# An adaptive-norm transformer block with routed experts: query tiles of the two rows interleaved, small vectors loaded as rows and turned, and the last results gathered by blocks

## What is computed

```python
mod = (silu(c) @ wmod).reshape(2, 6, 1, -1)      # per row: sa, ca, ga, sb, cb, gb
h = layernorm(x) * (1 + ca) + sa
x = x + ga * attn(h)     # layernorm(h)*gamma+beta, q k v, causal softmax, o_proj, + h
h = layernorm(x) * (1 + cb) + sb
probs = softmax(h @ w_router); top_w, top_i = top_k(probs, 4)   # of 16 experts
moe = sum over the 4: top_w * ((silu(h @ we1[e]) * (h @ we3[e])) @ we2[e])
shared = (silu(h @ ws1) * (h @ ws3)) @ ws2
x = x + gb * (shared / 5 + moe * 4 / 5)
```

## Time and profile before

| | |
|---|---|
| median of 3 runs | 345.75 us (345.56 to 346.32) |
| the profiled execution | 346.29 us, of which the span of the trace is 344.2 us |
| busy: PE, PEld, DVE, ACT, POOL | 324.0, 299.7, 255.5, 196.4, 204.3 us |
| the chain that ended last, by engine | PE 59%, DVE 20%, issue 9%, DMA 4%, POOL 4%, ACT 3% |
| DMA | 57.55 MB, mean 167 GB/s |

### The profile page before, as it was taken

The page is one execution under the profiler, slowest core; times in us unless marked ns, Lnnn a source line. Parts: engine busy times, 40 slices in busy tenths (PEclk is TensorE's granted clock), DMA queues, the critical chain, the costliest instruction groups (busy, mean ns, idle before and its releaser), DMA issues.

```text
span 344.2 us, 7783 instructions
## 1 busy us (share of the span) xinstructions
PE 324.0 (94%) x2298; PEld 299.7 (87%) x2298; DVE 255.5 (74%) x793; ACT 196.4 (57%) x439; POOL 204.3 (59%) x278
## 2 busy tenths in 40 slices
PE   6988999998889999999999988999999999999994
PEld 4787899998778999988878878999999999998883
DVE  1889999889978887466898756665656666669696
ACT  2467878775676855665443315666666666666210
POOL 1578855431787867467778401666666666667710
PEclk9999999999999999999999999999999999999999
DMA  6414920000112269773222165777776664989755
GB/s 214 154 50 171 288 94 18 15 17 17 70 69 91 100 193 349 234 236 121 103 103 105 70 170 141 236 230 228 228 223 195 195 208 152 292 316 389 239 194 169
DMA packets 43353, 57.55 MB, mean 167 GB/s; under 512 B 6225, under 2 KB 35665, under 8 KB 43313
## 3 DMA queue, kind: packets, MB, share of 16 engines
q1 hardware_dynamic: 35360, 35.42, 34.3%
q0 software_dynamic: 6864, 19.80, 15.1%
q10 hardware_dynamic: 1088, 1.84, 1.6%
HBM read 32.64 MB, written 24.40 MB: 166 GB/s over the span
## 4 chain that ended last, share of the span: by engine, by line
PE 59%; DVE 20%; issue 9%; DMA 4%; POOL 4%; ACT 3%; DVEq 0%; SPq 0%; POOLq 0%; ACTq 0%
PE ps L1697 14%; PE ps L1698 13%; PE ps L1699 13%; PE ps L1860 5%; PE ps L2061 5%; PE ps L2087 2%; POOL y_rows L733 2%; DVE bn L1116 2%; DMA cols<-in_L_c_dram 1%; DMA y_in<-y_rows 1%; DVE negmax L1516 1%; DVE y_in L1390 1%; PE ps L1965 1%; DVE y_in L1400 1%; DMA y_rows<-y_sb,aside 1%
## 5 line engine op out<-in xcount | busy, mean ns | idle before, releaser
L733 POOL DMA_INDIRECT y_rows<-y_sb,aside x79 | 79.9, 1012 | 54.5 <-ACT y_sb L1004 41.1
L698 POOL DMA_INDIRECT xg_rows<-hrow,slot_u x64 | 67.0, 1047 | 20.8 <-issue 17.8
L1697 PE MATMUL ps<-rpool 128*128 128x256 f32 (+3 forms) x164 | 51.9, 316 | 5.0 <-DVE rpool L1141 3.1
L1699 PE MATMUL ps<-rpool 128*128 128x256 f32 (+3 forms) x164 | 48.1, 293 | 0.0
L1698 PE MATMUL ps<-rpool 128*128 128x256 f32 (+3 forms) x164 | 48.0, 293 | 0.0
L1697 PE MATMUL ps<-w_hi_routed,xT_hi 128*128 x158 | 45.2, 286 | 1.9 <-DVE xT_lo L1633 1.8
L1699 PE MATMUL ps<-w_hi_routed,xT_lo 128*128 x158 | 44.7, 283 | 0.0
L1698 PE MATMUL ps<-w_lo_routed,xT_hi 128*128 x158 | 44.7, 283 | 0.0
L1697 PEld LDWEIGHTS ps<-rpool 128*128 128x128 f32 x164 | 31.2, 190 | 8.4 <-DVE rpool L1141 5.2
L995 ACT ACTIVATE r_silu<-ps 128x256 f32<-128x256 f32 x40 | 15.3, 383 | 36.7 <-PE ps L1699 35.7
L1697 PEld LDWEIGHTS ps<-w_hi_routed,xT_hi 128*128 128x128 f32 x158 | 30.2, 191 | 2.7 <-issue 2.6
(11 more groups left out here) (225 smaller groups left out, 928.6 us busy)
## 6 DMA issues: line engine op xcount, KB each, us to landing
xs<-xg_rows SPq DMA_DIRECT2D x68, 144.0 KB
y_in<-y_rows SPq DMA_DIRECT2D x16, 512.0 KB, 6.6
xg_rows<-empty SPq DMA_DIRECT2D x4, 576.0 KB, 3.3
x_in<-in_L_attn_x_dram SPq DMA_DIRECT2D x16, 128.0 KB, 2.3
w_raw_routed<-in_L_ffn_we_dram SPq DMA_DIRECT2D x8, 256.0 KB, 5.6
out_dram<-x SPq DMA_DIRECT2D x16, 128.0 KB, 1.8
xs_own<-xg_rows SPq DMA_DIRECT2D x11, 144.0 KB
wmod_sb<-in_L_wmod_dram ACTq DMA_DIRECT2D x3, 512.0 KB, 5.6
```

The lines of the kernel that those rows point to most:

```text
L698: nc.gpsimd.indirect_dma_start(out=xg, out_offset=bass.IndirectOffsetOnAxis(ap=slot_u[:, t, k:k + 1].bitcast(U32), axis=0), in_=hrow[:, t, ...
L733: nc.gpsimd.indirect_dma_start(out=yb, out_offset=bass.IndirectOffsetOnAxis(ap=dest[:, 2 * n + i:2 * n + i + 1].bitcast(U32), axis=0), in_ ...
L1697: nc.tensor.matmul(dst, w[0], x_[0], start=first, stop=False)
L1699: return nc.tensor.matmul(dst, w[1], x_[0], start=False, stop=last)
```

## The change

1. **Order.** A table `ORDER` maps positions to tiles: tile 8 now stands at position 6 and tile 9 at position 8, and tiles 6 and 7 move to positions 7 and 9. Everything that was written by tile is written by position with `row_of`, `index_of`. Keys and values now lie in three blocks of four tiles, so scores need one run of keys a block; before, the second row's keys lay in two runs. The second row's gate steps move: `gate_a(1)` from round 3 to 2, `wvo_gate(1)` from 4 to 3, `wvo_split(1)` from 6 to 4 (on ACT from 5 to 4). The token numbers of POOL become eight iotas in round 5 instead of one in round 3.
2. **Start.** c is loaded as four rows of 128 numbers, gamma and beta as two rows each; PE turns them with a 4 by 4 identity into PSUM, ACT takes silu from there, and copies gamma and beta to `cols`. `silu_b` and its five DVE instructions are gone: the modulation's weights are `silu_c` broadcast. The warm-up is four matmuls of a constant before c, and two behind it. Tile 0 of x is loaded ahead of qkv. DVE takes the first norm's statistics before the modulation and `wT_copy` after the first centring.
3. **Register reads.** PE's three `load_experts` go behind `gate_up` 9, 10 and 11. SP's marks, now 28, are read one behind each row load from pair 4 on.
4. **Fourth place by blocks.** The marks get three more lines: where expert 15's rows of groups 0, 1 and 2 end. Loads of the fourth place run block 0 to 3, and blocks 0, 1 and 2 wait only for the group in which their last tile lies. This costs DVE some steps in `route_marks` and PE one matmul in `tile_places`.
5. **Own buffers.** The results of pairs 36 to 39 go to `y_own`, so ACT doesn't wait there; POOL waits instead for the store of four pairs earlier.
6. **Last stores.** The last block is stored by two DMAs of two tiles.

```diff
+ORDER = (0, 1, 2, 3, 4, 5, 8, 6, 9, 7, 10, 11, 12, 13, 14, 15)
+AT = tuple(ORDER.index(tile) for tile in range(TILES))
...
+GROUP_OF = [max(AT[b * BT:(b + 1) * BT]) // BT for b in range(NB)]
+ENDS = TOPK + NG - 1
+def end_of_place(k, b):
+    if k < TOPK - 1 or GROUP_OF[b] == NG - 1:
+        return k
+    return TOPK + GROUP_OF[b]
...
+        V_HI = (Bq - RP, 0, Bq - RP + 1024)
+        xnT_hi = r_part(Bq - RP + 6144, 3072).rearrange("p (b c t) -> p b c t", b=3, c=DC)
...
+        def y_of(n):
+            if n < NPAIR - RING:
+                return y_sb[:, n % RING]
+            return y_own[:, n - (NPAIR - RING)]
...
         def _(sp):
-            with nc.allow_non_contiguous_dma(reason="small column loads"):
-                sp.dma_start(cols[:, 2:2 + B, :], c_in.rearrange("b (c p) -> p b c", p=P)).then_inc(s_ld_c, 16)
+            sp.dma_start(rows_c[:], c_in.rearrange("b (c p) -> (b c) p", p=P)).then_inc(s_ld_c, 16)
...
+            token_tile(0)
             sp.dma_start(qkv_sb[:], qkv.rearrange("(c p) n -> p c n", p=P)).then_inc(s_ld_qkv, 16)
-            token_tile(0)
...
+            token_tile(1)
+            sp.dma_start(rows_gb[0:DC, :], gamma.rearrange("(c p) -> c p", p=P)).then_inc(s_ld_cols, 16)
...
-            sp.wait_ge(s_marks, 1)
-            counts = [[sp.value_load(marks[0:1, k, r:r + 1], min_val=32, max_val=16 * loads_of(NPAIR - RING + r))
-                       for r in range(RING)] for k in range(TOPK)]
+            counts = {}
+            def fetch_count(m):
+                k, r = divmod(m, RING)
+                if m == 0:
+                    sp.wait_ge(s_marks, 1)
+                counts[k, r] = sp.value_load(marks[0:1, k, r:r + 1], min_val=32,
+                                             max_val=16 * loads_of(NPAIR - RING + r))
...
                 load_rows(n, place[2 * (n % 8):2 * (n % 8) + 2], s_xs[n % RING])
+                if 0 <= n - RING < RING * ENDS:
+                    fetch_count(n - RING)
...
             for k in range(TOPK):
-                for r in range(RING):
-                    sp.wait_ge(s_back[r], counts[k][r])
-                for b in (3, 0, 1, 2):
+                for b in (3, 0, 1, 2) if k < TOPK - 1 else range(NB):
+                    if b == 3 or k == TOPK - 1:
+                        for r in range(RING):
+                            sp.wait_ge(s_back[r], counts[end_of_place(k, b), r])
...
-                for t in range((2 * NB - 2 + i) * BT // 2, (2 * NB - 1 + i) * BT // 2):
-                    sp.dma_start(out_t[t], x1[:, t, :]).then_inc(s_out, 16)
+                two = slice((2 * NB - 2 + i) * BT // 2, (2 * NB - 1 + i) * BT // 2)
+                sp.dma_start(out_t[two].rearrange("t p d -> p t d"), x1[:, two, :]).then_inc(s_out, 16)
...
                 pool.wait_ge(s_ry, n + 1)
+                if n >= NPAIR - RING:
+                    pool.wait_ge(s_back[r], 16 * loads_of(n - RING))
...
-            act.wait_ge(s_ld_c, 16)
-            nc.scalar.activation(silu_c[:], cols[:, 2:4, :], ACT.Silu).then_inc(s_siluc, 1)
+            act.wait_ge(s_turned, 1)
+            nc.scalar.activation(silu_c[:], ps[:, 3, D:D + B * DC].rearrange("p (b c) -> p b c", b=B), ACT.Silu
+                                 ).then_inc(s_siluc, 1)
...
-                if n >= RING:
+                if RING <= n < NPAIR - RING:
                     act.wait_ge(s_back[r], 16 * loads_of(n - RING))
...
-            modulation1(0)
             stats1(0)
             stats_end(1, 0, "u")
+            modulation1(0)
+            norm1_centred(0)
             wT_copy()
-            norm1_centred(0)
...
+                if s == 2:
+                    gate_a(1)
                 if s == 3:
-                    gate_a(1)
+                    wvo_gate(1)
                 if s == 4:
-                    wvo_gate(1)
-                if s == 6:
                     wvo_split(1)
...
-                    last = nc.tensor.matmul(dst, silu_b[:, b, c, :], wmod_sb[:, c, n0:n1], start=(c == 0),
+                    last = nc.tensor.matmul(dst, silu_c[:, b, c:c + 1].broadcast_to((P, P)), wmod_sb[:, c, n0:n1],
...
+            pe.wait_ge(s_eps, 1)
+            turning(4)
+            pe.wait_ge(s_const, 4)
+            pe.wait_ge(s_ld_c, 16)
+            rows_turned(rows_c, 0)
+            turning(2)
+            pe.wait_ge(s_siluc, 1)
             pe.wait_ge(s_ld_wmod[0], 16)
             modulation(ps[:, 0, :], 0, 2 * D, 0).then_inc(s_mod1_mm, 1)
...
+                if n == UNITS_FIRST - HELD // 8:
+                    pe.wait_ge(s_places, 3)
+                if n >= UNITS_FIRST - HELD // 8:
+                    first = 8 * (n - UNITS_FIRST) + HELD
+                    load_experts(first, first + 8, first)
```

More of the change, by code:

```diff
@@ L773, in _ @@
                                  ).then_inc(s_wt_a, 1)
+            act.wait_ge(s_turned, 2)
+            nc.scalar.activation(cols[:], ps[:, 3, D + B * DC:D + B * DC + 2 * DC].rearrange("p (w c) -> p w c", w=2),
+                                 ACT.Copy).then_inc(s_gamma_beta, 1)
             act.wait_ge(s_wqk_mm, 1)
@@ L1919, in _ @@
                             done(pe, "x1", t - 2)
-                        for off, slot, n in key_runs(row0 + first, row0 + end):
-                            masked = own and first + off + n == end
-                            keys = slice(slot * P, (slot + n) * P)
-                            for c in range(DC):
-                                last = split3(dst[:, off * P:(off + n) * P],
-                                              (qT_hi[:, t % 2, c, :], qT_lo[:, t % 2, c, :]),
-                                              (xnT_hi[:, c, keys], xnT_lo[:, c, keys]), c == 0,
-                                              c == DC - 1 and not masked)
+                        four, keys = slot_of(row0 + first) // BT, slice(0, (end - first) * P)
+                        for c in range(DC):
+                            last = split3(dst[:, keys], (qT_hi[:, t % 2, c, :], qT_lo[:, t % 2, c, :]),
+                                          (xnT_hi[:, four, c, keys], xnT_lo[:, four, c, keys]), c == 0,
+                                          c == DC - 1 and not own)
                         if own:
@@ L2013, in last_logits, with load_experts @@
                        ).then_inc(s_lg_mm, 1)
+            HELD = 24
+            expert = [nc.alloc_register(PE_ENGINE, f"expert{n}") for n in range(2 * HELD)]
+            def load_experts(first, end, to):
+                pe.load(expert[2 * to:2 * (to + end - first)], places[0:1, 2 * NTL + 2 * first:2 * NTL + 2 * end])
             transpose_back(TILES - 2)
@@ L2037, in _ @@
             gate_up(UNITS_FIRST)
-            HELD = 24
-            expert = [nc.alloc_register(PE_ENGINE, f"expert{n}") for n in range(2 * HELD)]
-            def load_experts(first, end, to):
-                pe.load(expert[2 * to:2 * (to + end - first)], places[0:1, 2 * NTL + 2 * first:2 * NTL + 2 * end])
             def experts_of(n):
@@ L2100, in rows_down @@
                 last.then_inc(s_rdown, 1)
-            pe.wait_ge(s_places, 3)
-            for first in range(0, HELD, 8):
-                load_experts(first, first + 8, first)
             down(UNITS_FIRST - 1, range(0, BT // 2))
```

278 lines of the change are left out of this document (152 added, 126 removed).

## The result

| | before | changed |
|---|---|---|
| median of 13 runs each, side by side | 346.32 us (344.99 to 348.83) | 344.79 us (342.70 to 345.52) |
| ratio, 95% interval | | 0.994 (0.992 to 0.996) |
| profiled execution, its span | 346.29, 344.2 us | 345.19, 343.5 us |

The change is 1.5 us faster between medians, 2.1 us by the ratio. 344.79 lies in the predicted range; the gain is between half and three quarters of the 2.85 us that were forecast. The thirteen runs fall into two groups: five between 342.70 and 343.33 us at a mean granted clock of 0.995 to 1.00, eight between 344.75 and 345.52, all at 0.995. That the median lies in the range is in part luck: the range is over 5 us wide, and of the 2.9 us that were added up only the part behind attention came as worked out.

A forecast was written before the change was run, and what follows sets the result against it. PE was taken as the bound, 324.0 us busy. Start -0.7, attention -1.0, reads -0.45, end -0.85 and marks matmul +0.1 sum to -2.9: from 345.75 to a 342.9 us median, range 340.1 to 345.3.

The forecast's parts named there:

- the -1.5 that I had as the bound: Start: forecast -0.7 us, doubling to -1.5 if wmod also came earlier because c no longer stood in its way.
- the late clock: Rival at the start: modulation and transposes begin at the lower clock, about +1.5 us, +3.3 in full; 344.4 us, chance 0.13.
- matmuls of 1 us: Start: modulation matmuls this long were named as a sign that the forecast was wrong.
- It leaves the later one, so 0 on balance: Attention: `wvo_split(1)` and its gates come two rounds earlier, may push positions 3 to 5 but leave the later window; 0.
- The -1.0 for the order: Attention, positions 6 to 11: the new tile order balances PE and DVE, -1.0 us, between -3.6 and +2.8.
- the three waits of the earlier trace: Attention: PE waits three times, 2.9 us, for DVE's low parts of values and queries; one wait's price gave -1.0.
- The rival of the uncovered routing: Rival, positions 6 to 11: PE runs dry while DVE chooses and counts, windows lose 2.8 us; 346.65 us, chance 0.10.
- the 5.5 from which I let it decide: Positions 6 to 11: the slower rival decides once PE idles more than 5.5 us in those two windows.
- Reads -0.45: Behind attention: PE's three register reads moved behind `gate_up` 9 to 11, -0.45 us, bounds 0 and -0.8.
- where I had put 0.1: Path to the expert tables: the added matmul for the marks costs +0.1 us.
- End -0.85: End: 0.45 us from DVE's wait for the fourth place, 0.4 from two stores fewer; bounds -0.2 and -1.2.
- both were put at 0: Pairs 36 to 39: own buffers ending ACT's wait for a store, and POOL's new wait, were each put at 0.

The follow-up runs named there:

- warm53: Changed kernel with five warm-up matmuls before the transpose of c and three behind it, instead of four and two; median 342.55 us, 0.9887 of the kernel before.
- w_gate: `warm53` with DVE computing the second row's gate from PSUM before round 0, not in round 2; median 341.63 us, 0.9869 of the kernel before.
- again: The changed kernel run once more, unedited, as the base of the runs beside it; median 345.03 us, 0.9946 of the kernel before.
- fill: Changed kernel plus, in round 8, three constant matmuls before the normed input's transposes and seven before the first group's rank; median 344.48 us, 0.9944 of the kernel before.
- best: `w_gate` plus two constant matmuls before the normed input's transposes in round 8 and three before the rank; median 341.24 us, 0.9833 of the kernel before.

## Why the prediction was half right

**The start: the loads right, the sum wrong.** With c as rows wmod came 1.06 us earlier, and the modulation started 1.62 earlier, a little past the -1.5 that I had as the bound. The case that I held apart as a rival, the late clock, came with it and took 1.77 in the modulation (I had put 1.5), and the sign that I named for it, matmuls of 1 us, is there: 3.75 us for four. The sum has no place for that rival, yet the earlier the data, the less warm-up stands before it. `warm53` shows both parts. The rule of the Trainium skill (DMA: Bandwidth & Descriptors, Rules for kernel authors) that transfers issued from SP and ACT share the same 16 engines would, as I applied it, have kept wmod where it was. The trace does not agree with that use of it: 5.3 us to landing became 4.2. qkv and x stood beside wmod in both kernels, so the rule itself is not tested. What differs is the small packets: from 2 to 4.6 us the trace before has 445 under 512 B and moves 153 GB/s, the changed one 26 and 258. That the pieces of c held wmod back is argued from this, as no run changes the loads alone. The other rule of the Trainium skill (TensorE: Matmul & The Clock Gate, Part 1), that activity releases the clock at a point that varies, agrees: with the same warm-up the modulation took 3.04 us in one profile and 1.95 in another.

**Attention: the failed step.** "It leaves the later one, so 0 on balance" was wrong. I weighed `wvo_split(1)`, 0.69 us, which enters the window of positions 3 to 5, and not the 1.52 us of `gate_a(1)`, which stood in that window before and after and only moved one position to the front, before low parts that PE waits for. Positions 3 to 5 grew by 1.45, and `w_gate` gave that back whole.

The -1.0 for the order had the wrong place. In the two windows it was too much: they grew by 0.81 with the fall of the clock, and are 0.25 (`warm53`, 45.21) to 0.40 us (`w_gate`, 45.06) under the 45.46 of the earlier trace rows without it. DVE's low parts of values and queries no longer hold PE there, but the routing does in their stead (0.87 us). I read the three waits of the earlier trace rows as waits of these windows; one of them is that of position 12, and with it the order wins some 2 us in positions 12 to 15, where I had put nothing. POOL, whose scatters delay the norms there, I had left out. Together with the early gate the order is worth 2.7 us.

**The clock behind position 8: not foreseen.** The rival of the uncovered routing had the right place and the wrong price. PE idles 1.87 us in three gaps behind position 8, for ACT's `hrow` (0.66), while DVE chooses (0.87, listed as "issue") and for DVE's low parts (0.34); in the two windows it idles 3.13 of 46.27 us, less than the 5.5 from which I let it decide. What I did not price is that TensorE may then run at its lower level for 3.2 us. By the windows of `again` and `warm53` that costs 1.5 us, and ten of twelve runs of `again` have the lowered mean; `fill` and `best` kept the clock in 18 of 18.

**The rear: right.** Reads -0.45, measured 0.61 when put back; of this the first profile shows -0.10, because the path to the expert tables grew by 0.28 where I had put 0.1 (PE's first matmul that reads `tv` starts 44.54 us after position 15, before 44.26), while from there to pair 1 it takes 0.38 less. End -0.85, measured -0.96, and 1.46 when put back. ACT's wait for a store (2.7 us) went from the list of waits, and POOL's new wait does not show in it; both were put at 0, and neither was tried alone.

What stays open: why some runs of a kernel fall and others not (the profile of `warm53` has the same gaps of 0.66, 0.87 and 0.34 us, and its clock stays), and why the kernels with the longer warm-up fall more rarely than the changed one. The profile holds one run of each.

## What to carry to other kernels

When work moves earlier, follow every instruction of it to the place where it lands, and look at what stands behind it in that engine's queue and who waits for that; a window of three positions was too wide to show it here. When work moves from one stretch to another, look at every engine that has a fixed amount to do per round there, POOL's scatters here. A gap on TensorE costs its length and possibly the clock behind it, so a few matmuls of a constant in a gap that can't be closed are cheap if they stand ahead of the wait and end before it does. Data that comes earlier at the start is worth only what the engine's clock makes of it; lengthen the warm-up up to the moment at which the data is there.

## What the hardware showed that was not expected

The granted clock of the profile reads 1.00 in the first 9 us of the changed kernel, while the modulation's matmuls take twice their later time (3.75 us for four, 1.95 at full speed in `w_gate`): at the start one goes by durations. The trace's own records of the clock begin only at 8.87 us there, with the upper level (in the kernel before at 4.59), so the 1.00 ahead of them is no reading; the modulation's slow matmuls end at 8.93. In the changed kernel PE's gaps of 0.66, 0.87 and 0.34 us within 5.6 us were followed by 3.2 us at half clock, none of them longer than the 1.24 us gap at 42.41, behind which the clock stayed.
